# Relative attention, its opening: the loads in the order of use, the clears on VectorE, the constant product behind the first table

## What is computed

```python
dist = jnp.clip(idx[None, :] - idx[:, None], -R, R) + R      # R = 64
pe_k = rel_emb_k[dist]
pe_v = rel_emb_v[dist]
qkv = (x @ W_qkv + b_qkv).reshape(b, s, 3, H, hd)             # 16 heads of 16
...
score = jnp.einsum('bhqd,bhkd->bhqk', q, k) + jnp.einsum('bhqd,qkd->bhqk', q, pe_k)
attn = jax.nn.softmax(score, axis=-1)
ctx = jnp.einsum('bhqk,bhkd->bhqd', attn, v) + jnp.einsum('bhqk,qkd->bhqd', attn, pe_v)
...
return ctx @ W_out + b_out
```

## Time and profile before

| | us |
|---|---|
| median of 3 runs (lowest to highest) | 2228.03 (2219.94 to 2230.42) |
| the profiled execution, its time | 2227.24 |
| its span on the core | 2225.5 |
| mean granted TensorE clock, share of full speed | 0.861 |

### The profile page before, as it was taken

The page is one execution under the profiler, slowest core; times in us unless marked ns, Lnnn a source line. Parts: engine busy times, 40 slices in busy tenths (PEclk is TensorE's granted clock), DMA queues, the critical chain, the costliest instruction groups (busy, mean ns, idle before and its releaser), DMA issues. The chain is left out here.

```text
span 2225.5 us, 34942 instructions
## 1 busy us (share of the span) xinstructions
PE 1780.4 (80%) x12702; PEld 1362.7 (61%) x12702; DVE 1267.2 (57%) x3817; ACT 694.9 (31%) x1455; POOL 290.5 (13%) x259
## 2 busy tenths in 40 slices
PE   5889984799855468888886999678789879969958
PEld 4677764466534356666664466467667667757747
DVE  3465542355524145556563134534995996896896
ACT  3333320255534145555552111103402401411410
POOL 1434432000000300000001012300100100100100
PEclk9999987899976679999997855587889989979979
DMA  2000001000011168898884300060000000000000
GB/s 103 6 20 11 6 10 64 24 21 22 16 39 52 63 252 319 289 325 288 314 294 145 73 0 15 24 276 10 1 1 21 1 1 21 1 1 21 1 1 10
DMA packets 97317, 175.91 MB, mean 79 GB/s; under 512 B 16596, under 2 KB 81620, under 8 KB 92372
## 3 DMA queue, kind: packets, MB, share of 16 engines
q1 hardware_dynamic: 97140, 173.56, 22.5%
HBM read 93.72 MB, written 79.69 MB: 78 GB/s over the span
## 5 line engine op out<-in xcount | busy, mean ns | idle before, releaser
L2428 PE MATMUL bank<-per_up,per_act_w 128*128 128x256 f32 x1024 | 250.3, 394 | 0.0
L95 PE MATMUL bank<-per_xT,per_down 128*128 128x256 f32 x1024 | 223.6, 379 | 0.0
L95 PEld LDWEIGHTS bank<-per_xT,per_down 128*128 128x128 f32 x1024 | 194.7, 190 | 33.1 <-issue 7.6
L2428 PEld LDWEIGHTS bank<-per_up,per_act_w 128*128 128x128 f32 x1024 | 190.9, 194 | 23.2
L2344 DVE TENSOR_TENSOR per_hot_x<-per_picksT,per_iota_x 128x4096 f16<-128x4096 f16 x64 | 146.0, 2282 | 0.0
L1444 DVE CUSTOM_DVE_ANT_0 rel_summed<-bank,rel_bias 128x256 f32<-128x256 f32 x256 | 93.0, 422 | 63.0 <-PE bank L1550 45.7
L2249 ACT ACTIVATE per_act_w<-bank 128x512 f32<-128x512 f32 x128 | 76.4, 597 | 153.7 <-PE bank L95 153.6
L2441 PE MATMUL bank<-per_hot_y,per_hot_x 128*128 128x32 f16 x2048 | 71.0, 180 | 65.3 <-DVE per_act_w L2358 54.9
L2441 PEld LDWEIGHTS bank<-per_hot_y,per_hot_x 128*128 128x128 f16 x2048 | 66.9, 98 | 86.8 <-DVE per_hot_y L2349 65.0
L1362 ACT ACTIVATE rel_probs<-rel_summed,rel_low 128x256 f32<-128x256 f32 x256 | 114.0, 518 | 11.8 <-DVE rel_low L1444 11.8
L95 PE MATMUL bank<-ret_x2T,ret_w_in 128*128 128x256 f32 x384 | 97.9, 415 | 15.3 <-DVE ret_x2T L437 15.3
(11 more groups left out here) (346 smaller groups left out, 3539.6 us busy)
## 6 DMA issues: line engine op xcount, KB each, us to landing
rel_qr_rows<-rel_qr SPq DMA_DIRECT2D x32, 1024.0 KB, 7.0
rel_p_rows<-rel_probs SPq DMA_DIRECT2D x32, 1024.0 KB, 5.1
rel_bias<-rel_qr_rows SPq DMA_DIRECT2D x64, 384.0 KB, 4.4
rel_by_dist<-rel_p_rows SPq DMA_DIRECT2D x64, 384.0 KB, 4.7
per_down<-in_per_down SPq DMA_DIRECT2D x1, 4096.0 KB, 24.4
per_up<-in_per_up SPq DMA_DIRECT2D x1, 4096.0 KB, 33.7
ret_xin<-in_x SPq DMA_DIRECT2D x8, 256.0 KB, 2.8
x_after_ret<-ret_yout SPq DMA_DIRECT2D x8, 256.0 KB, 2.1
```

What stands on the lines that cost most here:

```text
L95: last = pe.matmul(dst, wt[:, c], src[:, c, :], start=c == 0, stop=c == DC - 1)
L2428: last = pe.matmul(tiles(bank[OUT_BANK[u]])[:, t, :], act_w[:, u, k, t * P:t * P + P], up[:, k, :], start=k == 0, stop=k == COLS - 1)
```

## The change

- `own` becomes two more columns of `cols`; the host lays out `reach_k`, `near_v` and `base_v` ready for one load each. So 22 set-up loads become 10.
- They are issued in the order of use after input batch 0, under four semaphores: `ident_loaded`; `loaded` (`cols`, `wq`, `wk`, `reach_k`); `wv_loaded`; `late` (`near_v`, `base_v`, `bo`, `wo`). Input batches 1 to 5 come behind.
- GpSimd keeps the clear of `band_v`. VectorE clears, ahead of its first step, those parts of `qr`, `v`, `bias` and `probs` that nothing else writes.
- `consts` is split into `bq_ready` (for ScalarE), `band_ready` (for the first table) and `const_in_ready` (for the product).
- The constant product stands behind the table of unit 0 and goes to bank 7; `const_row` is made at the end of VectorE's step -3; the first `values` waits for it.

```diff
-    cols, bo = sb("cols", [8]), sb("bo", [D])
+    cols, bo = sb("cols", [10]), sb("bo", [D])
     bq, bk, bv, far_v = cols[:, 0:2], cols[:, 2:4], cols[:, 4:6], cols[:, 6:8]
-    own, minus_own, bq_own = sb("own", [2]), sb("minus_own", [2]), sb("bq_own", [2, DC])
+    own, minus_own, bq_own = cols[:, 8:10], sb("minus_own", [2]), sb("bq_own", [2, DC])
...
-    zero = w["ext_v"].shape[0] // 2
-    loads = [(ident[:], ident_in), (cols[:], w["cols"]), (bo[:], w["bo"].partition_broadcast(P)),
-             (own[:], w["own"]), (wq[:], w["wq"]), (wk[:], w["wk"]), (wv[:], w["wv"]), (wo[:], w["wo"])]
-    loads += [(reach_k[a * HD:a * HD + HD], w["ext_kT"][:, zero - P + 1:zero + P]) for a in range(P // HD)]
-    loads += [(near_v[0:P - 1, 0], w["ext_v"][zero - REACH + 1:zero + REACH]),
-              (near_v[P - 1:P, 0], w["ext_v"][zero - REACH:zero - REACH + 1]),
-              (near_v[0:1, 1], w["ext_v"][zero + REACH:zero + REACH + 1]),
-              (near_v[1:P, 1], w["ext_v"][zero - REACH + 1:zero + REACH])]
-    loads += [(base_v[:, t], w["ext_v"][row:row + 1].partition_broadcast(P))
-              for t, row in ((0, zero + REACH), (1, zero - REACH))]
+    loads = [(cols[:], w["cols"]), (wq[:], w["wq"]), (wk[:], w["wk"]), (reach_k[:], w["reach_k"])]
+    late_loads = [(near_v[:], w["near_v"]), (base_v[:], w["base_v"].partition_broadcast(P)),
+                  (bo[:], w["bo"].partition_broadcast(P)), (wo[:], w["wo"])]
...
-            for b in range(2):
-                sp.dma_start(xin[:, b], batch_of(x_in, b)).then_inc(x_loaded[b], 16)
+            sp.dma_start(xin[:, 0], batch_of(x_in, 0)).then_inc(x_loaded[0], 16)
+            sp.dma_start(ident[:], ident_in).then_inc(ident_loaded, 16)
             load_all(sp, loaded, loads)
-            for b in range(2, XS):
+            sp.dma_start(wv[:], w["wv"]).then_inc(wv_loaded, 16)
+            load_all(sp, late, late_loads)
+            for b in range(1, XS):
                 sp.dma_start(xin[:, b], batch_of(x_in, b)).then_inc(x_loaded[b], 16)
...
-            pool.memset(qr[:], 0.0)
-            pool.memset(probs[:], 0.0)
-            pool.memset(bias[:], 0.0)
-            pool.memset(v[:], 1.0)
             pool.memset(band_v[:], 0.0)
...
-            pool.tensor_tensor(bq_own[:], bq.unsqueeze(1).broadcast_to([P, 2, DC]), over(minus_own[:], DC), ALU.mult)
+            pool.tensor_tensor(bq_own[:], bq.unsqueeze(1).broadcast_to([P, 2, DC]), over(minus_own[:], DC), ALU.mult)\
...
+                last = pool.tensor_scalar(band_k[:, t], reach_k[:, REACH * t:REACH * t + BAND],
+                                          reach_k[:, far:far + 1], None, ALU.subtract)
+            last.then_inc(band_ready, 1)
+            pool.wait_ge(late, 16 * len(late_loads))
             pool.tensor_tensor(band_v[:, :, 0:HD], near_v[:], base_v[:], ALU.subtract)
-            pool.drain()
             for t in range(TT):
                 last = pool.tensor_scalar(const_in[:, t], over(bv, P), far_v[:, t:t + 1], None, ALU.add)
-            last.then_inc(consts, 1)
+            last.then_inc(const_in_ready, 1)
             pool.wait_ge(const_ready, 1)
...
             act.wait_ge(loaded, 16 * len(loads))
-            act.wait_ge(consts, 1)
+            act.wait_ge(bq_ready, 1)
...
-            dve.wait_ge(loaded, 16 * len(loads))
-            dve.wait_ge(const_mm, 1)
-            dve.tensor_tensor(const_row[:], tiles(bank[0]), bo[:].unsqueeze(1).broadcast_to([P, TT, D]), ALU.add)\
-                .then_inc(const_ready, 1)
+            dve.memset(qr[:, :, :, BAND:BAND + P], 0.0)
+            dve.memset(qr[:, :, :, 2 * BAND + P:ROW], 0.0)
+            dve.memset(v[:, :, :, :, HD:VW], 1.0)
+            dve.memset(bias[:, :, 0, :, NEAR:SEQ], 0.0)
+            dve.memset(bias[:, :, 1, :, 0:REACH], 0.0)
+            dve.memset(probs[:, :, :, SEQ:WIDE - SEQ], 0.0)
+            dve.drain()
...
+                if table_of(s) == 0:
+                    dve.wait_ge(late, 16 * len(late_loads))
+                    dve.wait_ge(const_mm, 1)
+                    dve.tensor_tensor(const_row[:], tiles(bank[7]), bo[:].unsqueeze(1).broadcast_to([P, TT, D]),
+                                      ALU.add).then_inc(const_ready, 1)
...
-            pe.wait_ge(loaded, 16 * len(loads))
-            pe.wait_ge(consts, 1)
-            for t in range(TT):
-                for c in range(DC):
-                    last = pe.matmul(tiles(bank[0])[:, t], const_in[:, t, c], wo[:, c], start=c == 0, stop=c == DC - 1)
-            last.then_inc(const_mm, 1)
-            pe.wait_ge(const_ready, 1)
+            pe.wait_ge(ident_loaded, 16)
+
+            def constants():
+                pe.wait_ge(late, 16 * len(late_loads))
+                pe.wait_ge(const_in_ready, 1)
+                for t in range(TT):
+                    for c in range(DC):
+                        last = pe.matmul(tiles(bank[7])[:, t], const_in[:, t, c], wo[:, c], start=c == 0,
+                                         stop=c == DC - 1)
+                last.then_inc(const_mm, 1)
...
             def table(U, s):
                 b = U // GROUPS
+                if U == 0:
+                    pe.wait_ge(band_ready, 1)
...
             def values(U):
                 b, g = U // GROUPS, U % GROUPS
+                if U == 0:
+                    pe.wait_ge(const_ready, 1)
...
                 if (U := table_of(s)) is not None:
                     table(U, s)
+                    if U == 0:
+                        constants()
...
                     pe.wait_ge(xT_ready, b + 1)
+                    if b == 0:
+                        pe.wait_ge(loaded, 16 * len(loads))
                     for k, wt, done in ((0, wq, q_mm), (1, wk, k_mm)):
                         for g in range(DC):
                             last = project(pe, tiles(bank[k])[:, g], wt[:, :, g * P:g * P + P], xT[:, b % 2])
                         last.then_inc(done, 1)
+                    if b == 0:
+                        pe.wait_ge(wv_loaded, 16)
                     by_token(pe, tiles(bank[2]), xT[:, b % 2], wv).then_inc(v_mm, 1)
...
         "rel_cols": np.concatenate([column(by_rows(b[:D])), column(by_rows(b[D:2 * D])), column(b[2 * D:]),
-                                    np.tile(g("rel_emb_v")[[-1, 0]].T, (P // HD, 1))], 1),
-        "rel_bo": g("b_out"), "rel_own": own_rows(),
-        "rel_ext_kT": np.ascontiguousarray(extended(g("rel_emb_k")).T),
-        "rel_ext_v": extended(g("rel_emb_v")),
+                                    np.tile(g("rel_emb_v")[[-1, 0]].T, (P // HD, 1)), own_rows()], 1),
+        "rel_bo": g("b_out"),
+        "rel_reach_k": np.ascontiguousarray(np.tile(ext_k[zero - P + 1:zero + P].T, (P // HD, 1))),
+        "rel_near_v": np.stack([np.concatenate([span, ext_v[zero - half][None]]),
+                                np.concatenate([ext_v[zero + half][None], span])], 1),
+        "rel_base_v": ext_v[[zero + half, zero - half]],
```

12 lines of the change are left out of this document (8 added, 4 removed).

## The result

The changed kernel takes a median of 2211.73 us (19 runs, 2206.38 to 2225.83). The kernel before, run beside it, takes 2222.75 us (19 runs, 2215.7 to 2236.02). The ratio is 0.9953, with a 95% interval of 0.9935 to 0.9970: faster by 6.7 to 14.4 us, the middle at 10.4. The forecast was 2209.7 us and 18.3 us of gain. The absolute number is met within 2 us, the gain is not: 19 runs put the kernel before at 2222.75, where the three shown before the prediction had 2228.03. Part of the agreement is that starting point.

A forecast was written before the change was run, and what follows sets the result against it. The layer's hollow opening was taken to wait for the last of 22 loads, issued late. Saving 18.7 us on loads, less 0.4 for the projections' clock and 0 for the product, gave 18.3 and 2209.7 us, range 2202.5 to 2220.

The forecast's parts named there:

- The loads: Layer's opening: `reach_k` lands 3.8 us after issue, `loaded` at 752.0, first projection at 753.3 against 771.99; saves 18.7 us.
- GpSimd and ScalarE: Opening, after `loaded`: `bq_ready` at 752.6, ScalarE starts at about 752.7, first projection 0.65 us later.
- The clears: VectorE in the opening: 4.0 to 6.2 us of clears, done by 752 or 752.5, cost nothing with 8 us of cover.
- The clock of the projections: TensorE's three opening projections: without the product ahead they start colder, a loss of 0.4 us (bounds: loss 4.1, gain 1.5).
- The product: Constant product behind the first table: 3.0 to 5.0 us, hidden by the wait for the skewed read; cost 0, at most 1.
- The sum: Whole kernel: 18.7 - 0.4 - 0 = 18.3 us saved, giving 2209.7 us, 0.8% faster.
- Cold and late: Opening: slow load queue and projections at 1.2 GHz throughout; gain only 11 to 14 us, 2215; chance 0.2.
- It doesn't start earlier: Opening: `loaded` still lands with everything behind it, near 757.7; gain 13 us, or no change at 2228; chance 0.07.
- Slower: Layer's body: TensorE's granted clock falls from 0.92 to 0.85, costing 28 us, 2238; chance 0.03.
- What would show it wrong: Changed layer: `minus_own` starting after 755, TensorE waiting at the product, or the body growing by more than 5 us.

The follow-up runs named there:

- the delayed kernel: The changed kernel with 24.7 us of clears of an idle tile on GpSimd ahead of `minus_own`: 2235.58 us, ratio 1.0027 to the kernel before.
- with the new arrays: The kernel before, its 22 set-up loads reading the changed kernel's input arrays, run twice: 2226.64 us (ratio 1.0002) and 2227.25 us (1.0008).
- with all arrays: The changed kernel with the three old input arrays kept unused beside the new ones, code unchanged: 2214.93 us, ratio 0.9950 to the kernel before.

## Why the prediction was right, and where it was not

**How far the number was luck.** The measured 2211.73 us lie 2.0 above the forecast, but behind that stand two misses of opposite sign: the time that it started from was 5.3 us too high, and the gain was 7.3 too large (18.3, where the two medians give 11.0). A gain of 18.3 lies outside the measured 6.7 to 14.4. The terms for the opening add up nearly as forecast; what failed is the term that the sum has at nothing, everything behind the opening ("the body from the first bias on as long as before"). Some 5 to 6 us are given back there (below).

**The loads: right.** Four executions of the changed kernel start the first projection 7.1, 7.1, 7.1 and 7.4 us into the layer, four of the old opening 26.2, 25.9, 25.9 and 26.0. That is a shift of 18.9, where the forecast had 18.7. The landing of `reach_k`, taken at 3.8 us behind its issue between 2.8 and 6.0, is 3.35 here and at most 3.72 in the other profiles with that order of loads. Two amounts of data in the forecast are too small: with `reach_k` itself it is 1.0 MB and not 0.85, and up to input batch 5 it is 3.0 MB and not 2.4. Neither is a term of the sum.

**GpSimd and ScalarE: right.** From `minus_own` to the projection it takes 1.31 us here, 1.3 in the forecast.

**The clears: right.** 4.2 us of work in 4.7, in the range of 4.0 to 6.2, with a cover of 9 us.

**The clock of the projections: right in kind, too small.** The forecast was a loss of 0.4 us, 7.2 to 7.6, within −1.5 to 4.1. The windows of the changed kernel, its opening up to the first projection, and that projection:

```profile
749.40:756.50 7.10, 1.12 (x4) 0.72 (x4) 4.16 (x6) 0.60 (x1) 1.32 (x5) 0.50 0.77 197
756.50:759.70 3.20, 3.19 (x8) 2.61 (x9) 0.00 (x0) 0.00 (x0) 1.36 (x4) 0.55 0.86 278
```

The granted clock is 0.50, the lower level of 1.2 GHz, up to the first projection, and 0.55 in it; behind it the grant is 1.00. In the usual execution of the kernel before (here the second one), the product stood there, and the half speed fell on it (the product, then the three projections):

```profile
761.70:765.50 3.80, 3.75 (x8) 2.51 (x8) 0.00 (x0) 0.00 (x0) 0.00 (x0) 0.50 0.00 0
...
767.70:773.30 5.60, 5.45 (x24) 4.48 (x24) 0.05 (x1) 2.67 (x7) 0.71 (x1) 1.00 0.01 1
```

The product ran at 0.50 and the projections at 1.00. From the first projection to the first table it was 6.3 us in three executions and 8.0 in the one that I predicted from; now it is 7.7, 7.8, 7.8 and 9.3. The mean loss is 8.15 − 6.7 = 1.4 us, and 1.8 against the usual execution; against the one execution that the forecast started from the first three gain 0.2 to 0.3. The Trainium skill, "TensorE: Matmul & The Clock Gate", part 1 on the clock gate, says that the throttled state is the default and activity releases it; the pair of rows agrees. Two experiments bear on it. In the delayed kernel the projections start as late as they did before (26.4 us into the layer) but without the product, and it is 8.3 us from there to the first table, 2.0 more than in the usual execution with it. With the product put back, but early, it is 9.1: there the work in front gave nothing back.

**The product: right in effect, wrong in size.** 1.99 us, not 3.0 to 5.0: I had multiplied the duration of one record by eight, where records overlap. The 8 of a projection at full speed take 1.89, which stood in the earlier trace rows. The same slip made the product's 3.64 us before look only a little longer than the 3.03 of full speed, where it was nearly twice as long as the real full-speed time, and so made its part in the warm-up look small.

**The sum.** Against the one profile that it started from, the opening lost 20.0 us and not 18.3, since that execution had been the longest of its kind. Means over the four profiles of each kind (the kernel before twice and with the new arrays twice; the changed kernel three times and with all arrays once), by the starts of the layers in the timelines:

| us | old opening | new opening | difference |
|---|---|---|---|
| layer start to first table | 32.7 | 15.3 | −17.4 |
| opening, to the first bias | 45.8 | 28.0 | −17.8 |
| body of the layer | 416.2 (411.2 to 418.9) | 418.3 (414.6 to 422.3) | +2.1 |
| cross attention | 264.7 (263.7 to 267.3) | 266.4 (263.9 to 267.3) | +1.7 |
| loop of the last layer | 710.7 (706.5 to 716.1) | 712.9 (707.2 to 719.1) | +2.2 |
| span | 2223.9 | 2211.9 | −12.0 |

The opening gives what was forecast, 17.8 for 18.3. The whole gives 12, and the four ratios agree (0.9953, 0.9931, 0.9946, 0.9950: 10.4 to 15.4 us, the mean 12.2). Some 5 to 6 us are missing, spread over stretches whose code is unchanged. What such a stretch looks like, in the loop of the last layer: one of its four rounds in the kernel before, then two in the changed kernel:

```profile
1873.00:2048.00 175.00, 147.27 (x1076) 120.26 (x1077) 144.37 (x474) 41.80 (x64) 11.63 (x11) 0.92 0.03 8
```

```profile
1678.00:1855.00 177.00, 149.12 (x1076) 120.93 (x1076) 144.12 (x474) 41.80 (x64) 11.95 (x11) 0.91 0.03 8
1855.00:2034.00 179.00, 150.79 (x1078) 122.07 (x1079) 144.34 (x475) 41.80 (x64) 11.71 (x11) 0.90 0.03 8
```

The same 1076 to 1078 matmul records take 147 us of TensorE at a clock of 0.92 and 149 to 151 at 0.90 to 0.91, and a round takes 175 us or 177 to 179. It is the same in the body of the changed layer: over the eight profiles of the table TensorE's busy time in it goes from 334.3 to 344.8 us for the same 3124 records, and what is left of the body beside it is 76.4 to 77.9 us in all of them. So the body's length follows TensorE's busy time almost one for one. Each of the three rows of the table varies as much between executions of one kernel as it differs between the two kinds, so none of them is shown to be the place.

Whether the missing part belongs to the change is not settled. For it: the delayed kernel, whose opening is 1.7 us longer than the mean of the old ones, is 6.0 us slower (2.0 to 9.8). Against it: with the clears on GpSimd the opening is 9.2 us shorter than the old, and the ratio says 8.9 (5.6 to 12.0); with the product ahead it is 5.9 shorter, and the ratio says 6.9 (2.0 to 11.8). So a fixed price of the new order doesn't fit these two. A fixed share of the shift fits badly too: two thirds of the delay's 20.3 would be 14, where 21.4 were measured, uncertain by some 6 (against the mean of the four runs of the changed kernel it is 18, uncertain by some 4). What is left open is where TensorE's clock drops in the later layers, and whether it drops a little more in this kernel; whether the place of the code in memory plays a part was not tried by itself. Four profiles of each kind are too few for 2 us in stretches that vary by 8 to 12.

**The rivals.** *Cold and late* named the gain that was measured, 11 to 14, but not its mechanism: the loads were early, and two of three projections ran at full speed in three profiles of four, one of three in the fourth. *It doesn't start earlier* had `minus_own` near 757.7, 11.9 us into the layer; it ran 5.8 us in. *Slower* had the body's granted clock fall to 0.85: it was 0.91 to 0.94 in the new kernel and 0.92 to 0.94 in the old. But the clock behind the opening, which it pointed at, is what is seen to vary with the lengths of the stretches in which the rest was lost.

**What would show it wrong** was `minus_own` after 755, and it is at 755.20. That bound was given in the clock of the profile before, for a layer that starts at 745.8; this one starts at 749.38, and 5.8 us into the layer stands against 9.2. Such bounds are to be given from the layer's own start. TensorE has no wait at the product, and the body is at the most 3.4 longer than in the profile before (422.3 for 418.9), 2.1 in the mean of four. The layer ends 15.7 us earlier behind its start, on the average, and not 18.

None of the kernels tried beats the changed one.

## What to carry to other kernels

Where a layer's opening waits for loads, follow the wait to the last load that is really used, give it a semaphore of its own, and then clear the way behind it: here the loads alone would have run into GpSimd's clears (8.2 us of the opening) and into the product (10.9 us), and each part shows its full price in the opening only with the others in place. Work of TensorE that is taken away from in front of the first matmuls can take a warm-up away too (here 1.4 to 2.0 us), though putting it back earlier gave nothing; price that, and from more than one execution. And when a shift of the opening is clean, expect the whole to show it only to within what the clock does elsewhere: here 18 us of opening became 12 of kernel, and where the rest went is not shown.

## What the runs showed of the hardware that was not expected

- An unchanged layer has a few lengths, not one: the cross attention took 263.5 to 263.9 us in five profiles, 267.1 to 267.3 in seven and 270.8 in one, all with the same code. The body of the changed layer varies over 11 us (411.2 to 422.3), and so does TensorE's busy time in it (334.3 to 344.8), at a granted clock of 0.94 to 0.91.
- The first projection of the changed layer took 3.39 or 3.46 us in three executions and 3.78 in a fourth, with the same code and the old arrays kept beside the new; there the second took 3.13 in place of 1.89.
- VectorE clears at 0.87 to 0.89 ns for an element of a partition (1536 in 1.34 us, 1024 in 0.91), as fast as GpSimd (0.86).
- The write of 1 MB behind the first table let SP go on 3.86 us after its issue when the next table came 3.4 us later with regard to it (one execution); in the twelve other profiles it was 4.82 to 5.60. The cause is open.
